# The attention's output product in chunk order instead of tile order, on TensorE of one Trainium2 core

## What is computed

```
r, k, v = split(x @ W_rkv + b_rkv);  r = sigmoid(r);  k = exp(k)
u1, u2  = running sums over time of k*v and k, each decayed by lam per channel
att     = (u1 + gamma*k*v) / (u2 + gamma*k + 1e-6) * r
z       = layernorm(x + att @ W_o + b_o)
xr, xk  = mu * z + (1 - mu) * (z one token earlier), with mu_r and mu_k
out     = layernorm(z + sigmoid(xr @ W_r) * (relu(xk @ W_k)^2 @ W_v))
```

## Time and profile before

| | |
|---|---|
| median of 3 runs | 2523.39 us (2523.05 to 2524.15) |
| the profiled execution's own time | 2522.33 us |
| its span, first to last instruction | 2520.5 us |
| PE busy | 2505.9 us, 99% of the span |
| DVE busy | 2096.1 us, 83% |
| ACT busy / POOL busy | 1270.5 us, 50% / 1248.0 us, 50% |
| chain that ended last | PE 96%, DVE 1%, issue 1%, POOL 1% |
| mean granted clock of TensorE | 0.999 |
| DMA | mean 44 GB/s |

### The profile page before, as it was taken

The page is one execution under the profiler, slowest core; times in us unless marked ns, Lnnn a source line. Parts: engine busy times, 40 slices in busy tenths (PEclk is TensorE's granted clock), DMA queues, the critical chain, the costliest instruction groups (busy, mean ns, idle before and its releaser), DMA issues.

```text
span 2520.5 us, 32920 instructions
## 1 busy us (share of the span) xinstructions
PE 2505.9 (99%) x11263; PEld 2074.6 (82%) x11263; DVE 2096.1 (83%) x2693; ACT 1270.5 (50%) x2157; POOL 1248.0 (50%) x1130
## 2 busy tenths in 40 slices
PE   9999999999999999999999999999999999999998
PEld 6888888888888888888888888888888888888877
DVE  8888888888888888888888888888888888888884
ACT  5554455545455454554445544455544455454545
POOL 5744445454554544545445444455454554545544
PEclk9999999999999999999999999999999999999999
DMA  4001111111011111111111111101111111111100
GB/s 180 17 34 51 51 34 34 42 44 51 34 45 40 35 51 41 44 34 35 51 51 34 34 35 51 51 34 34 35 50 51 34 43 40 37 51 34 51 26 34
DMA packets 57784, 110.63 MB, mean 44 GB/s; under 512 B 7040, under 2 KB 7040, under 8 KB 57088
## 3 DMA queue, kind: packets, MB, share of 16 engines
q1 hardware_dynamic: 56736, 108.03, 12.6%
q10 hardware_dynamic: 864, 0.28, 0.1%
HBM read 74.73 MB, written 33.55 MB: 43 GB/s over the span
## 4 chain that ended last, share of the span: by engine, by line
PE 96%; DVE 1%; issue 1%; POOL 1%; DMA 0%; ACT 0%; POOLq 0%; DVEq 0%
PE bankB L1204 14%; PE bankB L1206 13%; PE bankB L1205 13%; PE bankA L1183 13%; PE bankA L1185 13%; PE bankA L1184 13%; PE bankB L1251 4%; PE bankB L1253 4%; PE bankB L1252 4%; PE bankB L1229 2%; DVE att_f L946 0%; POOL xk_lo L456 0%; DMA wrkv_f<-in_w_rkv 0%; PE bankA L1206 0%; PE bankA L1205 0%
## 5 line engine op out<-in xcount | busy, mean ns | idle before, releaser
L1183 PE MATMUL bankA<-x_hi,wrkv_hi 128*128 128x512 f32 x1488 | 583.2, 392 | 3.5 <-POOL x_lo L424 3.5
L1185 PE MATMUL bankA<-x_hi,wrkv_lo 128*128 128x512 f32 x1488 | 580.0, 390 | 0.0
L1184 PE MATMUL bankA<-x_lo,wrkv_hi 128*128 128x512 f32 x1488 | 579.8, 390 | 0.0
L930 DVE RECIPROCAL gate<-gate 128x512 f32<-128x512 f32 x128 | 429.2, 3353 | 4.4
L429 POOL TENSOR_TENSOR att_f<-att_f,gate 128x512 f32<-128x512 f32 x128 | 207.3, 1620 | 278.1 <-DVE att_f L951 278.1
L1183 PEld LDWEIGHTS bankA<-x_hi,wrkv_hi 128*128 128x128 f32 x1488 | 279.8, 188 | 61.6 <-POOL x_lo L424 3.9
L1185 PEld LDWEIGHTS bankA<-x_hi,wrkv_lo 128*128 128x128 f32 x1488 | 279.7, 188 | 58.5
L1184 PEld LDWEIGHTS bankA<-x_lo,wrkv_hi 128*128 128x128 f32 x1488 | 279.8, 188 | 57.6 <-issue 0.5
L456 POOL TENSOR_TENSOR xk_lo<-xk_f,xk_hi 128x512 fp32r<-128x512 f32 x124 | 177.3, 1462 | 239.7 <-ACT xk_hi L714 239.7
L706 ACT ACTIVATE z<-z,shift,rstd 128x512 f32<-128x512 f32 x124 | 94.4, 809 | 361.3 <-POOL shift L449 361.3
L440 POOL TENSOR_TENSOR ve<-mv,eps_ln 128x2 f32<-128x2 f32 x126 | 65.6, 521 | 390.2 <-DVE mv L963 385.7
(11 more groups left out here) (161 smaller groups left out, 5609.8 us busy)
## 6 DMA issues: line engine op xcount, KB each, us to landing
y<-in_x SPq DMA_DIRECT2D x126, 256.0 KB, 2.7
x_f<-in_xT SPq DMA_DIRECT2D x124, 256.0 KB, 3.9
out<-z SPq DMA_DIRECT2D x124, 256.0 KB, 2.0
wrkv_f<-in_w_rkv SPq DMA_DIRECT2D x3, 768.0 KB, 9.0
xk_f<-in_xT SPq DMA_DIRECT2D x4, 256.0 KB, 5.6
wo_f<-in_w_o SPq DMA_DIRECT2D x1, 1024.0 KB, 12.4
wr_f<-in_w_r SPq DMA_DIRECT2D x1, 1024.0 KB, 15.0
wv_f<-in_w_v SPq DMA_DIRECT2D x1, 1024.0 KB, 18.0
```

What stands on the lines that cost most here:

```text
L930: dve.reciprocal(gate[:, c % 2], gate[:, c % 2]).then_inc(rec_made, 1)
L1183: pe.matmul(bank[:], w_hi, hi[:, h], start=(h == 0), stop=False)
L1184: pe.matmul(bank[:], w_hi, lo[:, h], start=False, stop=False)
L1185: last = pe.matmul(bank[:], w_lo, hi[:, h], start=False, stop=(h == NC - 1))
```

## The change

In `step`, and only there, the two calls of `attention_out` give way to four calls of a new function, `attention_part(s1, c)`, one for each chunk. The chunk is now the outer loop and the tile the inner one. Chunk 0 waits until all four sums are begun. Each chunk waits for its own `att_lo` (before, tile 0 waited for all). The four `ready["WO"]` signals come in the last chunk, one after each tile. The matmuls are the same, with the same operands and banks. `finale` keeps `attention_out` for the last two blocks. No other engine's program changes.

```diff
+            def attention_part(s, c):
+                if c == 0:
+                    pe.wait_ge(sum_begun, s.count(NT, NT))
+                if s.first():
+                    pe.wait_ge(w_lo_made[W_WO], NC - 1)
+                if s.first() and c == NC - 1:
+                    pe.wait_ge(att_made, NC)
+                elif s.first():
+                    pe.wait_ge(att_first_lo, c + 1)
+                else:
+                    pe.wait_ge(att_lo_made, s.count(NC, c + 1 - NC))
+                if s.second() and c == 0:
+                    pe.wait_ge(w_lo_made[W_WO], NC)
+                for tile in range(NT):
+                    bank, rows = psum_of(s, "WO", tile), slice(tile * P, (tile + 1) * P)
+                    if s.first() and c == NC - 1:
+                        last = pe.matmul(bank[:], att_f[:, c, rows], wo_f[:, c], start=False, stop=True, skip_group_check=True)
+                    else:
+                        pe.matmul(bank[:], att_hi[:, c, rows], wo_hi[:, c], start=False, stop=False, skip_group_check=True)
+                        pe.matmul(bank[:], att_hi[:, c, rows], wo_lo[:, c], start=False, stop=False, skip_group_check=True)
+                        last = pe.matmul(bank[:], att_lo[:, c, rows], wo_hi[:, c], start=False, stop=(c == NC - 1),
+                                         skip_group_check=True)
+                    if c == NC - 1:
+                        last.then_inc(ready["WO"], 1)
+
@@ step, after project(s, 1, 0)
-                attention_out(s1, 0)
-                attention_out(s1, 1)
+                attention_part(s1, 0)
+                attention_part(s1, 1)
+                attention_part(s1, 2)
+                attention_part(s1, 3)
                 project(s, 1, 1)
```

## The result

| | before | changed |
|---|---|---|
| median of 11 runs | 2523.32 us | 2530.25 us |
| lowest to highest | 2522.43 to 2524.15 | 2529.74 to 2530.77 |
| profiled execution, its own time | 2522.33 us | 2530.14 us |
| span | 2520.5 us | 2528.3 us |

The ratio is 1.0028, with a 95% interval of 1.002 to 1.0035. The changed kernel is 6.9 us slower.

What follows compares the result with a forecast made beforehand. PE, busy 2505.9 of 2520.5 us, was taken as the bound, so only its waits cost. Six stalls of 1.13 us, 6.8 us, other terms 0, on 2523.39 gave 2530.2 us, range 2524.5 to 2535.

Steps and rivals of the forecast that it cites:

- the forecast case: PE stalls for the fourth sum in the six steps behind the loop's jumps, 6.8 us in all; chance 65%.
- Matmuls and bank changes: The product's 48 matmuls in each of 30 steps cost the same in the new order: 0, with 2 us for the range.
- The finer waits: Each chunk waiting for its own `att_lo` gains nothing, since PE had no wait for `att_lo` to shorten: 0.
- The joint wait in ordinary steps: At the product's start the fourth sum is ready 0.41 to 2.33 us early, so PE does not wait: 0.
- The stall: PE at the product behind each jump: 0.93 lateness, 0.05 to the matmul, 0.10 first matmul, 0.05 register instruction; 1.13 us.
- The late signals: Later `ready["WO"]` signals delay DVE's statistics by 0.1 us at most at the end; 2.17 us cover at PE's transposes: 0.
- Rival 1: Behind the jumps DVE's standstill is really shorter, the fourth sum is in time, no change: 2523.4 us; chance 24%.
- The threshold that I worked out: DVE's standstill at a jump below which PE never waits for the fourth sum: 1.6 us.
- Rival 2: PE's clock falls at each stall behind a jump: 17 us in all, 2540.4 us; chance 4%.
- Rival 3: The late first half of the statistics delays the keys in 24 ordinary steps: 8.9 us more, 2539.1 us; chance 5%.
- PE's busy time: A sign in the changed profile: PE's busy time over the program stays unchanged.
- some 6 us: A sign: PE's new waits for DVE's sum (L977) behind the jumps, six of 0.8 to 1.2 us each.

## Why the prediction was right

Forecast 2530.2 us, measured 2530.25; the forecast case, six stalls behind the jumps, is what happened. That the two agree to 0.1 us is chance. The lateness of a sum differs between executions (0.82 to 1.05 us in the kernel before, 0.64 to 1.02 with a wait for each tile), PE's own loss at a jump, up to 0.38 us, is in no term, and the median of before differs by 0.2 us between the chips. An agreement within some 1 us is what the working can claim.

- *Matmuls and bank changes, 0 with 2 us kept.* Right: the chunk order with a wait for each tile is at 1.0001, and the product takes 10.65 us in both orders. (The first of the 30 steps has 44 rows of matmuls in the trace and not 48, in both kernels alike.)
- *The finer waits, 0.* Right. The product never waits for `att_lo` in either trace, so nothing was there to win.
- *The joint wait in ordinary steps, 0.* Right: the six waits are all behind jumps. The narrowest of the loop's ordinary steps has 1.73 us to spare in the changed kernel.
- *The stall, 1.13 us, six times 6.8.* The trace gives 1.14 and 6.86. The terms inside shifted: from the sum's end to the matmul it is 0.13 to 0.14 in all six, where I had 0.05 and 0.05 for the register instruction, together 0.10. The 0.10 of the first matmul behind a wait stands, and the matmuls behind it bring another 0.03. The lateness against an undisturbed start of PE is 0.89 on average, for 0.93.
- *The late signals, 0 behind a cover of 2.17 us.* Right, and sized right: DVE waits 0.67 us (forecast 0.75), the statistics end at 11.88 (forecast 11.8 to 11.9), the cover at the transposes is 2.06. The steps behind a jump in the trace of before had shown the same timing.
- *Rival 1, a shorter standstill at the jump.* It did not hold: the changed kernel shows 15.1 us over six jumps, the kernel before 14.5. That it is the jump that matters is shown by the written-out loop. The threshold that I worked out, 1.6 us of standstill, is doubtful: it counts a microsecond of lateness for each of standstill, and a shorter standstill would also have spared some of the 1.75 us by which the first two sums are longer beside POOL. No run shows where the threshold lies.
- *Rival 2, the clock.* It does not fall at these stalls (mean granted clock 1.00 from 55 to 2525 us), as the granted clock of the changed kernel over the first one shows:

```profile
529.00:533.00 4.00, 3.20 (x14) 2.68 (x15) 3.86 (x6) 1.90 (x3) 0.00 (x0) 1.00 0.00 0
```

  The Trainium skill, "TensorE: Matmul & The Clock Gate", section "A second HAM failure mode: psum-queue depth-cycling", ties the swinging clock to frequent small idle times between groups of matmuls. That case does not arise here: the order that changes bank every three matmuls has no idle time between them, and without the joint wait it has the time of before. Idle time does pull the clock down at three times the length of these stalls, as the kernel with the earlier wait shows, and once at 1.9 us.
- *Rival 3, the keys.* Not there; the cover at the fourth chunk is 0.69 us.
- *What I said of the changed profile and was wrong in:* PE's busy time was to stay, and it rose by 3.8 us. None of it is more work. About 1.7 us of it lies ahead of the first product, with the longer slow stretch in it. The rest is in how a wait is counted: the stretch with the jumps is 6.86 us longer and the row of waits has 4.6, so 2.2 us pass as busy. For that row I had forecast "some 6 us" in waits of 0.8 to 1.2; it has 4.6 in waits of 0.6 to 0.9, because I did not take off the modelled end of the matmul before. And DVE's wait for PE ahead of L958, which I gave as a sign of the change, is no new row: the kernel before has it 23 times, 15.3 us, at the fourth tile. The changed kernel has it 29 times, 21.3 us; the six more stand behind the jumps, where PE's stall makes DVE wait 1.0 us.

## What to carry to other kernels

When several waits are gathered into one ahead of a group of work, look at the latest producer in the worst step and not in the usual one: here 24 of 30 steps had room, and the loss came from the six behind the loop's jump. A wait for each bank cost nothing here while it was satisfied, so leave it with the first instruction that needs it. The new order itself was free, since each operand kept a wait of its own and the later signals had cover (2.06 us at the transposes); check both before you change an order.

## What the runs showed of the hardware

- Waits of the same length on TensorE may or may not bring the clock down: of six waits of 3.46 to 3.65 us four did and two did not, in one execution. A wait of 1.9 us did in one execution and did not in another; 24 waits of up to 1.34 us and the changed kernel's six of 0.6 to 0.9 us did not.
- How long the clock then stays low differs too: for 7 to 12 matmuls there, and for 7 to 13 behind the wait of 3.5 to 3.9 us at the start, over the profiled executions. At 0.20 us each that is 1.2 us between executions of the same instructions, nearly half the spread of the runs of before (2.7 us).
- A sum of DVE (128x512, two operands) takes 0.69 to 0.82 us without POOL beside it and up to 1.86 us while POOL runs, in the kernel before.
- PE's own loss at a jump is between 0 and 0.38 us and differs from jump to jump and from execution to execution. It comes ahead of the first projection; with the loop written out it is not there.
- The first matmul behind a wait takes 0.33 us to the next start where others take 0.23, whatever the length of the wait (0.04 to 3.5 us), as long as the clock holds.
